# A graph kernel whose sum over three axes and scan terms move from TensorE to VectorE, with the turn of a batch reordered on ScalarE and TensorE

## The chip, the cores and the metric

The kernel runs on one core of one Trainium2 chip. The metric is the time of the whole program on the device in microseconds (us). A core has five engines that run side by side and wait for one another through semaphores: TensorE (PE: matmuls, and PEld for its weight loads), VectorE (DVE), ScalarE (ACT), GpSimd (POOL, which here issues the gathers) and SyncE (SP, which issues the other transfers). Each engine works through its own list of instructions in order.

## The reference

The reference has two layers on a graph of 12,500 nodes with 32 features and 200,000 edges, which are sorted by their destination `dst`.

```
x = layernorm(x + mean over the edges into a node of x[src])          # layer 0
R = relu(edge_weight * w1 + b1) @ w2 + b2                              # 384 numbers per edge
Y = spherical_harmonics(edge_attr_3)                                   # from the edge's direction
msg[e] = sum over (R, Y, features of src[e], constants)                # 8 scalars, 8 vectors of 3
x = layernorm(x + sum over the edges into a node of msg[e])           # layer 1
```

In layer 1 the 32 features of a node are 8 scalars and 8 vectors of three components, and so is a message. The kernel doesn't form `Y`. For each edge it has a rotation (`frame`, 3 by 3) that turns the edge's direction onto one axis. It rotates the gathered vectors into that frame, multiplies with `R` there, and rotates the message back. Rotating back is a sum over the three axes a of (message component a) times (row a of the frame).

## The kernel before

**Tiling.** The 200,000 edges lie as 128 partitions of 1564 edges; the columns are worked through in 98 batches (`BATCHES`) of `T` = 16 columns. A loop `layer1(i)` holds two batches, k = 0 and 1. Its batch is b. On each engine there is a function `layer1` that writes out by hand the order of its instructions for batch b, together with the rest of batch b-1 and the head start of batch b+1. Nothing else sets the order.

**A batch of layer 1.** GpSimd gathers the source nodes' features into `got[k]` (line 688), 16 gathers per batch. VectorE rotates them (lines 1659 to 1666) and ScalarE copies the scalars (842). TensorE transposes them (`turn_features`, 1002), ScalarE copies the result to `ft` (848), and TensorE spreads it in six steps (`spread_features`, 1018, S0 to S5). TensorE makes the radial numbers in six steps, always for the next batch (`radial`, 990, R0 to R5). All six use one pair of PSUM banks, `radial_slot`, so each waits until ScalarE has copied the last one to its SBUF room (`copy_radial`, 822). There is one room per step, and a room can be written again once VectorE has multiplied with it. VectorE multiplies in eight steps (`multiply`, 1645, m0 to m7). TensorE sums the products in four steps (`sum_products`, 1027).

**The turn of a batch.** After the last sum of batch b-1, ScalarE copies it to `summed_t` (`copy_summed`, 829), TensorE transposes it into the PSUM bank `messages` (`turn_messages`, 1037), VectorE copies the 8 scalars to `scalars_s` (1619) and makes the three products `back[a]` with the frame (`turn_back`, 1621). TensorE's `add_axes` adds the three by matmuls with the identity matrix (1043) and brings the scalars beside them (1045), into `terms2`. That is the same PSUM bank as `messages`, in another order: feature first, then column. VectorE adds the carry of the batch before (`carry`, 1437) and scans along the columns (`scan_terms`, 1442); ScalarE turns the runs (729), and they go to DRAM. On TensorE `add_axes` stands behind S0 and S1 and ahead of R1. On VectorE the scan stands between m3 and m4.

`Steps` numbers VectorE's own instructions: `mark` counts one, `settle` waits until all that were marked have ended. `STEPS` is the number of marks per turn of the loop. The line numbers are those of the kernel before.

Of the kernel before, what the change touches and what calls it, by code (L numbers as in the profile page):

```python
# [11 lines left out]
ALU = mybir.AluOpType  # L12
# [6 lines left out]
D = 32  # L19
MUL = 8  # L20
H = 64
RD = 6 * MUL * MUL
T = 16
COLS = 1568
CR = 1564
BATCHES = COLS // T
# [45 lines left out]
TL = CR - (BATCHES - 1) * T  # L72
# [15 lines left out]

STEPS = {"layer0": 8, "layer1": 16, "frames": 21}

# [15 lines left out]
def build_program(nc, x, src, dst, edge_attr, edge_weight, w1, b1, w2, b2, out):  # L106
    with ExitStack() as ctx:
# [3 lines left out]
        def sem(name):  # L111
            return ctx.enter_context(nc.semaphore(name))
# [93 lines left out]
        turned_in = [room[:, :, :, :, :].rearrange("p t a b v -> p t (a b v)") for room in f_along]  # L206
        scalars_s = f_across[1][:, :, :, :, :].rearrange("p t a b v -> p (t a b v)")[:, 0:T * MUL].rearrange("p (t u) -> p t u", u=MUL)
        summed_t = f_across[0][:, :, :, :, :].rearrange("p t a b v -> p (t a b v)")
# [67 lines left out]
        messages = ps_m[:, 0, :].rearrange("p (t o) -> p t o", o=D)  # L276
        terms2 = ps_m[:, 0, :].rearrange("p (o t) -> p o t", t=T)
        summed_p = ps_m[:, 1, :]
# [75 lines left out]
        back_ready = sem("back_ready")  # L354
        axes_summed = sem("axes_summed")
        frame_b_loaded = pair("frame_b_loaded")
# [348 lines left out]
        def _(act):  # L705
# [125 lines left out]
            def layer1(i, last=False):  # L831
                for k in range(2):
# [3 lines left out]
                    w = TL // QUAD * P if final else QUAD * P  # L836
                    if not first:
                        copy_summed(b - 1)
                    act.wait_ge(got2_landed[k], 16 * (T * i + n))
                    if not isinstance(b, int) or b > 1:  # L840
                        act.wait_ge(turned, b - 1)
                    act.copy(turned_in[k][:, 0:n, 0:MUL], got[k][:, 0:n, 0:MUL]).then_inc(f0_copied, 1)
                    copy_radial(b, UNITS - 1, w)
                    act.copy(idx[k][:, :], src_all[:, bass.ds((b + 2) * T, T)]).then_inc(idx_ready, 1)
                    act.wait_ge(turned, b + 1)
# [34 lines left out]
        def _(pe):  # L880
# [150 lines left out]
            def turn_messages(b, w=QUAD * P):  # L1031

                pe.wait_ge(summed_copied, b + 1)
                if not isinstance(b, int) or b > 0:
                    pe.wait_ge(scanned, BATCHES + b)
                for j in range(w // P):
                    mm = pe.transpose(ps_m[:, 0, j * P:(j + 1) * P], summed_t[:, j * P:(j + 1) * P], ident[:, :])  # L1037
                mm.then_inc(messages_ready, 1)

            def add_axes(b, n=T):  # L1040
                pe.wait_ge(back_ready, b + 1)
                for a in range(3):
                    pe.matmul(terms2[:, MUL:D, :].rearrange("p (u i) t -> p t i u", i=3)[:, 0:n], ident[:, :],  # L1043
                              back[:, a, 0:n], start=(a == 0), stop=(a == 2), skip_group_check=True)
                pe.matmul(terms2[:, 0:MUL, :].rearrange("p u t -> p t u")[:, 0:n], ident[:, :],
                          scalars_s[:, 0:n, :], start=False, stop=True, skip_group_check=True).then_inc(axes_summed, 1)

            def layer1(i, last=False):
                for k in range(2):
# [5 lines left out]
                    if not first:  # L1055
                        sum_products(b - 1, 3)
                        turn_messages(b - 1)
                    turn_features(b, k, w)
                    if not final:
                        radial(b + 1, 1 - k, 0, later)  # L1060
                    spread_features(b, k, 0, w)
                    spread_features(b, k, 1, w)
                    if not first:
                        add_axes(b - 1)
                    if not final:
# [32 lines left out]
            turn_messages(BATCHES - 1, TL // QUAD * P)  # L1098
            add_axes(BATCHES - 1, TL)

# [9 lines left out]
        def _(dve):  # L1110
# [499 lines left out]
            def turn_back(b, k, n=T):  # L1610

                dve.wait_ge(messages_ready, b + 1)
                if isinstance(b, int):
                    dve.wait_ge(frame_b_loaded[k], 16 * (b // 2 + 1))
                else:
                    dve.wait_ge(frame_b_loaded[k], 8 * (b - k + 2))
                if not isinstance(b, int) or b > 0:
                    dve.wait_ge(axes_summed, b)
                s.mark(dve.tensor_copy(scalars_s[:, 0:n, :], messages[:, 0:n, 0:MUL]))
                for a in range(3):  # L1620
                    ins = dve.tensor_tensor(back[:, a, 0:n], spread(messages[:, 0:n, MUL * (a + 1):MUL * (a + 2)], 2, 3),
                                            spread(frame_b[k][:, 0:n, :, a], 3, MUL), ALU.mult)
                    if a < 2:
                        s.mark(ins)
                ins.then_inc(back_ready, 1)

            def scan2(b, k):

                dve.wait_ge(axes_summed, b + 1)
                dve.wait_ge(masks2_ready, b + 1)  # L1630
                dve.wait_ge(runs_turned, BATCHES + b - 1)
                dve.wait_ge(scanned, BATCHES + b)
                carry(b, k, terms2)
                scan_terms(k, terms2)
# [69 lines left out]
```

## Time and profile before

| | |
|---|---|
| time, median of 3 runs | 3803.33 us (3798.77 to 3803.84) |
| profiled execution: its time | 3798.03 us |
| profiled execution: its span | 3796.3 us |
| TensorE busy | 3310.6 us (87%) |
| VectorE busy | 2762.8 us (73%) |
| GpSimd busy | 2786.3 us (73%) |
| ScalarE busy | 2061.5 us (54%) |
| mean granted clock of TensorE | 0.949 |

The span is the time from the first to the last instruction of the profiled execution. Busy shares are means over stages with different limits. Layer 0 with its nodes ends near 1590 us, layer 1's batches end near 3660 us, and the nodes of layer 1 follow. The clock is that granted to TensorE: 1.00 is 2.4 GHz, 0.50 is 1.2 GHz.

### The profile page before, as it was taken

What the parts mean: (1) busy time and instruction counts of PE and PEld (TensorE: products, weight loads), DVE (VectorE), ACT (ScalarE), POOL (GpSimd) and SP (SyncE); (2) the same over time, 40 slices, a digit from 0 to 9 for tenths busy, and PEclk for the clock granted to TensorE, in tenths of its full rate; (3) what the DMA queues carried; (4) which work ended last, traced back from release to release, by engine and by line L of the source; (5) the groups of instructions that cost most, each with busy time, mean ns of one, the idle gap of its engine ahead of it and who ended that gap; (6) DMA issues with size and microseconds to landing.
All of it is one profiled execution on the core that took longest, in us unless ns stands there. A gap on an engine that the chain in (4) does not pass through costs nothing.

```text
span 3796.3 us, 58108 instructions
## 1 busy us (share of the span) xinstructions
PE 3310.6 (87%) x17312; PEld 1902.1 (50%) x17312; DVE 2762.8 (73%) x3470; ACT 2061.5 (54%) x2391; POOL 2786.3 (73%) x2915
## 2 busy tenths in 40 slices
PE   4999999999999883399999999999999999999963
PEld 3898889898989783222323232333323232323232
DVE  5787877787878785467777777777777777777765
ACT  4777777776777660145454545454554545454520
POOL 6777777777777776677777777777777777777746
PEclk9999999999999995599999999999999999999975
DMA  4122222222122211122222222222222222222211
GB/s 100 39 57 41 52 43 43 50 44 54 40 55 43 50 48 29 39 57 53 62 55 59 55 59 55 59 58 56 62 52 62 55 59 54 59 55 59 57 28 26
DMA packets 188428, 197.65 MB, mean 52 GB/s; under 512 B 60241, under 2 KB 149427, under 8 KB 188085
## 3 DMA queue, kind: packets, MB, share of 16 engines
q1 hardware_dynamic: 95508, 149.13, 13.7%
q0 software_dynamic: 92832, 47.72, 9.7%
q14 instruction: 77, 0.63, 0.1%
q8 instruction: 11, 0.18, 0.0%
HBM read 134.02 MB, written 62.59 MB: 52 GB/s over the span
## 4 chain that ended last, share of the span: by engine, by line
PE 70%; ACT 12%; DVE 5%; POOL 5%; issue 5%; DMA 1%; SPq 0%; ACTq 0%; DVEq 0%; POOLq 0%
PE ps_r L940 19%; PE ps_r L990 17%; PE ps_m L1027 10%; PE ps_m L940 10%; PE ps_r L1018 8%; ACT prod_room L822 8%; POOL ngot L667 4%; DVE unit L1645 3%; PE ps_m L1037 2%; PE ps_r L1002 2%; ACT f_across L829 2%; PE ps_r L924 1%; ACT hot_s L739 1%; PE ps_m L1043 1%; ACT hot_s L742 1%
## 5 line engine op out<-in xcount | busy, mean ns | idle before, releaser
L688 POOL DMA_INDIRECT got<-x_d,idx x1564 | 1506.2, 963 | 530.6 <-issue 504.7
L822 ACT ACTIVATE prod_room<-ps_r,bias_col 128x1024 f32<-128x1024 f32 x392 | 435.9, 1112 | 780.0 <-PE ps_r L990 531.9
L940 PE MATMUL ps_r<-x_hi,hot_s 128*128 128x448 f32 x1974 | 741.6, 376 | 41.7 <-ACT hot_s L742 41.7
L1645 DVE TENSOR_TENSOR x_room<-radial_more,ps_r 128x1024 f32<-128x1024 f32 x392 | 475.0, 1212 | 384.0 <-PE ps_r L1018 252.3
L990 PE MATMUL ps_r<-hid,wc 64*128 64x512 f32 (+1 forms) x2352 | 669.8, 646 | 81.2 <-ACT prod_room L822 72.9
L940 PE MATMUL ps_r<-x_lo,hot_s 128*128 128x448 f32 x1974 | 733.0, 371 | 0.0
L739 ACT ACTIVATE hot_s<-rows,minus_row 128x512 fp32r<-128x512 f16 (+1 forms) x658 | 449.0, 764 | 244.0 <-PE ps_m L940 206.2
L1018 PE MATMUL ps_r<-ft,repeat 32*128 32x512 f32 (+1 forms) x2352 | 553.4, 639 | 1.1 <-ACT ft L848 0.6
L1645 DVE TENSOR_TENSOR unit<-prod_room,ps_r 128x1024 f32<-128x1024 f32 x392 | 451.1, 1213 | 106.9 <-PE ps_r L1018 102.0
L940 PEld LDWEIGHTS ps_r<-x_hi,hot_s 128*128 128x128 f32 x1974 | 378.3, 192 | 75.5 <-issue 43.0
L990 PEld LDWEIGHTS ps_r<-hid,wc 64*128 64x128 f32 x2352 | 178.8, 186 | 448.8 <-ACT prod_room L822 255.3
L940 PEld LDWEIGHTS ps_r<-x_lo,hot_s 128*128 128x128 f32 x1974 | 378.0, 192 | 32.7
L642 POOL DMA_INDIRECT got<-in_x_dram,idx_deep x322 | 310.5, 964 | 107.9 <-PE ps_r L940 42.7
L642 POOL DMA_INDIRECT f_across<-in_x_dram,idx_deep x331 | 314.3, 950 | 100.8 <-issue 42.0
L642 POOL DMA_INDIRECT f_along<-in_x_dram,idx_deep x326 | 315.0, 966 | 99.3 <-issue 40.2
L940 PE MATMUL ps_m<-x_hi,hot_s 128*128 128x448 f32 x987 | 362.0, 367 | 0.0
L940 PE MATMUL ps_m<-x_lo,hot_s 128*128 128x448 f32 x987 | 361.7, 366 | 0.0
L742 ACT ACTIVATE hot_s<-hot_s 128x3584 fp32r<-128x3584 f32 x94 | 336.1, 3576 | 3.0
L1018 PEld LDWEIGHTS ps_r<-ft,repeat 32*128 32x128 f32 x2352 | 148.0, 183 | 371.0 <-issue 150.3
L729 ACT COPY runs_t<-runs 128x512 f32<-128x512 f32 x196 | 210.0, 1071 | 133.8 <-DVE runs L1442 133.8
L667 POOL DMA_INDIRECT ngot<-run_d,pos x196 | 185.0, 944 | 111.5 <-issue 59.1
L1369 DVE TENSOR_TENSOR prod_room<-ps_r,hot_l 128x448 f32<-128x448 f32 x282 | 167.6, 620 | 118.8 <-PE ps_r L940 109.9
(203 smaller groups left out, 4438.4 us busy)
## 6 DMA issues: line engine op xcount, KB each, us to landing
hid<-weight_t SPq DMA_DIRECT2D x196, 256.0 KB
run_d<-runs_t SPq DMA_DIRECT2D x194, 256.0 KB
got<-x_d,idx POOLq DMA_INDIRECT x1564
rows<-code_d SPq DMA_DIRECT2D x47, 160.0 KB
frame_d<-x_sb SPq DMA_DIRECT2D x7, 1008.0 KB, 4.5
frame<-frame_d SPq DMA_DIRECT2D x98, 72.0 KB
frame_b<-frame_d SPq DMA_DIRECT2D x98, 72.0 KB
rows<-code_d SPq DMA_DIRECT2D x47, 128.0 KB
```

The costliest lines, as they stand in the source:

```text
L642: pool.indirect_dma_start(got_deep[k][:, t, :], None, x, bass.IndirectOffsetOnAxis(ap=idx_deep[q][:, k * T + t:k * T + t + 1], axis=0)).th ...
L667: pool.indirect_dma_start(ngot[c][:, j, :], None, table, bass.IndirectOffsetOnAxis(ap=pos[:, node_j:node_j + 1], axis=0)).then_inc(ngot_la ...
L688: pool.indirect_dma_start(got[k][:, t, :], None, x1_d, bass.IndirectOffsetOnAxis(ap=idx[k][:, t:t + 1], axis=0)).then_inc(got2_landed[k], 16)
L729: act.copy(runs_t[k][:, :, :], runs[k][:, :, :].rearrange("p f t -> p t f")).then_inc(done, 1)
L739: act.activation(hot_s[k][:, a, :, :], rows[k][:, :, :], ACT.Abs, bias=minus_row[:, a:a + 1]).then_inc(off_rows, 1)
L742: act.activation(hot_s[k][:, :, :, :], hot_s[k][:, :, :, :].bitcast(F32), ACT.Relu, bias=1.0, scale=-1.0).then_inc(hot_s_ready, 1)
L822: act.activation(radial_s[u][:, :, 0:w], radial_slot[:, :, 0:w], ACT.Identity, bias=bias_col[:, c:c + 1]).then_inc(radial_copied, 1)
L940: mm = pe.matmul(found[BANK_OF[k][g]], hot_s[k][:, a, g, :], part[:, a * LN * D:(a + 1) * LN * D], start=(a == 0 and n == 0), stop=(a == B ...
L990: mm = pe.matmul(radial_slot[:, t, 0:w], wc[half, c * P:(c + 1) * P], hid[k][half, :].rearrange("p (j c e) -> p j c e", c=2, e=P)[:, 0:w / ...
L1018: mm = pe.matmul(slot[:, t, 0:w], repeat[group, c, :], ft[group, 0:w], start=True, stop=True)
L1027: mm = pe.matmul(summed_p[t * D:(t + 1) * D, 0:w], to_feature[:, D - MUL - q * MUL:2 * D - MUL - q * MUL], product[q][t // 2][:, t % 2, 0: ...
L1645: dve.tensor_tensor(product[q][h][:, :, 0:w], radial_s[u][:, :, 0:w], spread_slot[(k + s_ + 1) % 2][:, :, 0:w], ALU.mult).then_inc(multipl ...
```

## The change

- `add_axes` goes. TensorE makes neither the sum over the axes nor the copy of the scalars, and the semaphore `axes_summed` goes with it.
- `terms2` moves from the PSUM bank to an SBUF tile (`f_across[1]`, which held `scalars_s`). VectorE copies the scalars into it directly, and adds the three products by two additions right behind them, ahead of m0. The second writes `terms2` with strides. Carry and scan read SBUF.
- The transpose of the messages waits for the products of the batch before (`back_ready`) instead of its scan.
- ScalarE: the copy of the sum (`copy_summed`) stands behind the copy of the scalar features and of the last radial step, instead of ahead of them.
- TensorE: R0 of the next batch stands ahead of both transposes, instead of behind them.

```diff
-STEPS = {"layer0": 8, "layer1": 16, "frames": 21}
+STEPS = {"layer0": 8, "layer1": 20, "frames": 21}
...
-        scalars_s = f_across[1][:, :, :, :, :].rearrange("p t a b v -> p (t a b v)")[:, 0:T * MUL].rearrange("p (t u) -> p t u", u=MUL)
+        terms2 = f_across[1][:, :, :, :, :].rearrange("p t a b v -> p (t a b v)").rearrange("p (o t) -> p o t", t=T)
...
-        terms2 = ps_m[:, 0, :].rearrange("p (o t) -> p o t", t=T)
...
@@ scalar, layer1
-                    if not first:
-                        copy_summed(b - 1)
                     act.wait_ge(got2_landed[k], 16 * (T * i + n))
...
                     act.copy(turned_in[k][:, 0:n, 0:MUL], got[k][:, 0:n, 0:MUL]).then_inc(f0_copied, 1)
                     copy_radial(b, UNITS - 1, w)
+                    if not first:
+                        copy_summed(b - 1)
                     act.copy(idx[k][:, :], src_all[:, bass.ds((b + 2) * T, T)]).then_inc(idx_ready, 1)
...
@@ tensor, turn_messages
                 if not isinstance(b, int) or b > 0:
-                    pe.wait_ge(scanned, BATCHES + b)
+                    pe.wait_ge(back_ready, b)
...
-            def add_axes(b, n=T):
-                pe.wait_ge(back_ready, b + 1)
-                for a in range(3):
-                    pe.matmul(terms2[:, MUL:D, :].rearrange("p (u i) t -> p t i u", i=3)[:, 0:n], ident[:, :],
-                              back[:, a, 0:n], start=(a == 0), stop=(a == 2), skip_group_check=True)
-                pe.matmul(terms2[:, 0:MUL, :].rearrange("p u t -> p t u")[:, 0:n], ident[:, :],
-                          scalars_s[:, 0:n, :], start=False, stop=True, skip_group_check=True).then_inc(axes_summed, 1)
...
@@ tensor, layer1
                     if not first:
                         sum_products(b - 1, 3)
+                    if not final:
+                        radial(b + 1, 1 - k, 0, later)
+                    if not first:
                         turn_messages(b - 1)
                     turn_features(b, k, w)
-                    if not final:
-                        radial(b + 1, 1 - k, 0, later)
                     spread_features(b, k, 0, w)
                     spread_features(b, k, 1, w)
-                    if not first:
-                        add_axes(b - 1)
                     if not final:
                         radial(b + 1, 1 - k, 1, later)
...
@@ vector, turn_back
-                if not isinstance(b, int) or b > 0:
-                    dve.wait_ge(axes_summed, b)
-                s.mark(dve.tensor_copy(scalars_s[:, 0:n, :], messages[:, 0:n, 0:MUL]))
+                s.mark(dve.tensor_copy(terms2[:, 0:MUL, :].rearrange("p u t -> p t u")[:, 0:n], messages[:, 0:n, 0:MUL]))
                 for a in range(3):
...
                 ins.then_inc(back_ready, 1)
+                s.settle()
+                s.mark(dve.tensor_tensor(back[:, 0, 0:n], back[:, 0, 0:n], back[:, 1, 0:n], ALU.add))
+                s.settle()
+                dve.wait_ge(back_ready, b + 1)
+                s.mark(dve.tensor_tensor(terms2[:, MUL:D, :].rearrange("p (u i) t -> p t i u", i=3)[:, 0:n],
+                                         back[:, 0, 0:n], back[:, 2, 0:n], ALU.add))
...
@@ vector, scan2
-                dve.wait_ge(axes_summed, b + 1)
                 dve.wait_ge(masks2_ready, b + 1)
+                s.settle()
```

## Rows read from the trace of the kernel before

**Rows 1.** The page: granted clock in 40 slices of the span, in tenths.
```profile
PEclk9999999999999995599999999999999999999975
```

**Rows 2.** One line's instructions (ns min/median/max, first and last start), and a group, 1900 to 3600.
```profile
L842 ACT COPY f_along<-got x81: 300/301/304, 1911.1 to 3582.3; 128x128 f32<-128x128 f32 x81
...
L688 POOL DMA_INDIRECT got<-x_d,idx x1307 | 1259.5, 964 | 441.0 <-issue 425.5 <-ACT f_along L842 15.5
```

**Rows 3.** Timeline, all engines, one batch: start, us, instructions, idle before and its releaser.
```profile
2516.40 0.56 DVE L1662 TENSOR_TENSOR part<-part 128x384 f32<-128x384 f32 x1
...
2517.07 0.65 PE L1037 MATMUL ps_m<-ident,f_across 128*128 128x128 f32 x4 [0.78 <-ACT f_across L829]
...
2518.13 1.47 DVE L1621 TENSOR_TENSOR back<-ps_m,frame_b 128x384 f32<-128x384 f32 x3
2518.26 1.13 PE L990 MATMUL ps_r<-hid,wc 64*128 64x512 f32 x4
2518.37 0.59 ACT L848 COPY ft<-ps_r 128x512 f32<-128x512 f32 x1
...
2519.32 1.14 PE L1018 MATMUL ps_r<-ft,repeat 32*128 32x512 f32 x8
...
2520.39 2.20 PE L1043 MATMUL ps_m<-back,ident 128*128 128x384 f32 x6
2520.66 4.61 DVE L1645 TENSOR_TENSOR unit<-prod_room,ps_r 128x1024 f32<-128x1024 f32 x4 [1.05 <-PE ps_r L1018]
...
2523.08 1.13 PE L990 MATMUL ps_r<-hid,wc 64*128 64x512 f32 x4 [0.27 <-ACT prod_room L822]
...
2524.34 1.11 ACT L822 ACTIVATE prod_room<-ps_r,bias_col 128x1024 f32<-128x1024 f32 x1 [1.31 <-PE ps_r L990]
...
2527.05 1.13 PE L990 MATMUL ps_r<-hid,wc 64*128 64x512 f32 x4
...
2535.01 1.13 PE L990 MATMUL ps_r<-hid,wc 64*128 64x512 f32 x4
...
2536.07 1.06 PE L1027 MATMUL ps_m<-x_room,to_feature 128*32 128x512 f32 x8
...
2537.28 0.59 ACT L829 COPY f_across<-ps_m 128x512 f32<-128x512 f32 x1 [2.33 <-PE ps_m L1027]
...
2537.99 0.65 PE L1037 MATMUL ps_m<-ident,f_across 128*128 128x128 f32 x4 [0.86 <-ACT f_across L829]
```

**Rows 4.** The chain that ended last, in order of time, two batches: start, us, what.
```profile
2521.92 1.12 ACT prod_room L822
...
2541.39 2.13 PE ps_m L1043 x6
```

**Rows 5.** Timeline, batch 0 of layer 1, TensorE.
```profile
1618.98 1.14 PE L1018 MATMUL ps_r<-ft,repeat 32*128 32x512 f32 x8
1622.70 2.08 PE L990 MATMUL ps_r<-hid,wc 64*128 64x512 f32 x4 [2.59 <-ACT prod_room L822]
...
1629.58 1.13 PE L990 MATMUL ps_r<-hid,wc 64*128 64x512 f32 x4
```

**Rows 6.** Groups of VectorE, 100 to 1600: busy us, mean ns of one, idle before.
```profile
L1413 DVE TENSOR_TENSOR x_sb<-unit,x_sb 128x224 f32<-128x224 f32 x7 | 4.2, 603 | 0.0
...
L1410 DVE TENSOR_TENSOR x_sb<-unit,x_sb 128x224 f32<-128x224 f32 x7 | 3.1, 437 | 0.0
```

**Rows 7.** Windows: length, busy of PE, PEld, DVE, ACT, POOL, granted clock, DMA share, GB/s.
```profile
1621.00:1622.00 1.00, 0.00 (x0) 0.00 (x0) 1.00 (x2) 0.46 (x1) 0.69 (x2) 0.99 0.04 5
```

**Rows 8.** Layer 0: timeline of TensorE, and windows (PE busy, clock, DMA share, GB/s).
```profile
1314.06 0.46 PE L940 MATMUL ps_r<-x_hi,hot_s 128*128 128x448 f32 x1 [2.98 <-ACT hot_s L742]
...
1314.00:1315.00 1.00, 0.94 (x4) 0.89 0.03 4
...
1318.00:1319.00 1.00, 1.00 (x6) 0.91 0.06 12
```

**Rows 9.** Timeline of GpSimd: one gather of layer 1.
```profile
2518.75 0.95 POOL L688 DMA_INDIRECT got<-x_d,idx  x1 [0.30 <-issue]
```

More of the change, by code:

```diff
@@ L354, in build_program @@
         back_ready = sem("back_ready")
-        axes_summed = sem("axes_summed")
         frame_b_loaded = pair("frame_b_loaded")
@@ L1098, in _ @@
             turn_messages(BATCHES - 1, TL // QUAD * P)
-            add_axes(BATCHES - 1, TL)
             pe.wait_ge(tail_ready[1], 1)
```

## The prediction

> **What bounds the kernel now.** I first read the page's line of the granted clock [rows 1]. It tells the stages apart: layer 0, a dip to half clock at the nodes, then layer 1, with the clock full from its second slice to its end. The diff touches layer 1 alone, so everything else is counted as unchanged. A tile that is copied once per batch gives the length of a batch: 80 steps between 1911.1 and 3582.3, 20.89 us each [rows 2]. Layer 1 has 98 batches. All but the last have another behind them, so I multiply by 97.
>
> Next comes the timeline of one batch [rows 3]. I measure from the start of the message transpose (M, line 1037) at 2517.07 to the next M at 2537.99, 20.92 us. R0 to R5 are the radial products (line 990), S0 to S5 the spreads (1018), m0 to m7 VectorE's multiplications (1645). R1 starts at M+6.01. R5 starts at R1+11.93, the last sum of products (line 1027) 1.06 behind it at R1+12.99, ScalarE's copy of that sum (829) at R1+14.20, and the next M at R1+14.91. The sum 6.01+14.91 gives the 20.92. TensorE is busy or one hop from busy nearly everywhere, so a reader of the page would call it the bound.
>
> The chain of waits shows what that hides [rows 4]. In one batch the way from S0 to R1 goes through m0 on VectorE and the radial copy on ScalarE; in the other it goes through the three axis matmuls. So two chains of equal length run between S0 and R1. R1 needs the PSUM slot that R0 filled; ScalarE empties it into the SBUF room that m0 must have read first. In [rows 3] this is S0 2519.32, m0 2520.66, R1 2523.08, with the copy at 2521.92 [rows 4] between them: 3.76 us. The axis matmuls lie wholly inside that wait. Batch 0 is the proof at hand: it has no axis matmuls, yet its S0 at 1618.98 is followed by R1 at 1622.70, 3.72 us, and TensorE stands idle 2.59 us in between [rows 5].
>
> **The change part by part.**
>
> *Axis matmuls and the scalars' matmul taken from TensorE.* They take from 2520.39 to about R1, 2.6 us, and leave 0 us of gain: 3.72 against 3.76. What was their place becomes an idle wait. S0 and S1 end about 1.07 us after S0's start (2519.32 to 2520.39).
>
> *R0 moved ahead of M, and ScalarE's last radial copy moved ahead of the copy of the sum.* In the kernel before, M waits for the sum's copy, until R1+14.91. In the new order R0 must first wait for ScalarE's copy of R5. From R1 (2523.08) its copy starts 1.26 later (2524.34) and takes 1.11. So R5's copy runs from R1+13.19 to R1+14.30, and R0 starts at R1+14.35. R0 and the next piece lie 1.06 apart (2518.26 to 2519.32), so M starts at R1+15.41. The sum's copy follows R5's on ScalarE, ends at about R1+14.9, and is covered. M is late by 15.41-14.91 = 0.50 us. Everything of the next batch hangs on M: the transposed messages start VectorE's part, whose m0 releases R1. The feature transpose queued behind M is late with it.
>
> *What the order gives back.* Without R0 between the feature transpose and S0, S0 starts once ScalarE has copied the features: M+1.30 (2518.37) plus 0.59 plus a hop of 0.12, as from the end of line 829 (2537.87) to M (2537.99). That is M+2.01 instead of M+2.25, and would allow m0 at M+3.35. But VectorE isn't free then.
>
> *Two additions on VectorE, and strided writes.* VectorE's three products start at M+1.06, in 1.48 us for three. I let the first addition start 0.06 before their end, M+2.48, since they overlap. It is of the kind and shape of line 1662, 0.56 us. It waits for the first to end; with an estimated hop of 0.06 the second starts at M+3.1. Its output is strided (64, 192 and 4 bytes in its loops), a form the layer doesn't have. Nearest are two multiplications of the frames with like inputs: 437 ns written densely, 603 with a stride [rows 6]. That is 0.74 ns for each of 224 elements; on 384 elements it is 0.28 us, so 0.84 us. The next instruction then starts some 0.08 before its end: m0 at M+3.86 instead of M+3.59, 0.27 us late. Bounds: dense price, 0 us; all 384 elements at the strided row's whole 2.7 ns each, 1.03 us, m0 0.46 late. The scalars' copy also gets a stride, at most 128 times 0.74 ns, which is inside that. I take 0.26. The old wait of VectorE before m0 (1.06 us) is what hides the rest; it is used up now. The scan reads SBUF instead of PSUM. It delays m4 at worst, which S2 doesn't wait for, so I give it nothing.
>
> The Trainium skill weighs against my stride price: "VectorE: DVE Perf Modes", section "The TRN2 errata", gives an fp32 tensor_tensor in SBUF as (N+151)/0.96 ns, 557 for 384 elements, with no term for strides. Row and formula agree for the dense form; by it alone the second addition costs 0.56 and the sum below falls by 26 us. "SBUF — State Buffer", section "Door 1: The DMA port swizzle", says on the other hand that each access to another 16-byte line pays, which the two rows of the frames bear out.
>
> *The clock.* Work done, R1 is now at M+6.01+0.26 = M+6.27, while S0 and S1 end at M+3.08. TensorE is idle for 3.2 us in every batch, and for 0.7 before S0. M's own wait, 0.86 us, is the longest of the batch before [rows 3]. Batch 0 shows what such a wait does: TensorE ran out of work at about 1620.1, the granted clock was at its upper level, 1.00 of 2.4 GHz, and fell at the end of the microsecond to 1622 [rows 7]. R1's four matmuls take 2.08 us there instead of 1.13, at 1.2 GHz; R2's at 1629.58 take 1.13 again [rows 5]. The same in layer 0: a wait of 2.98 us before 1314.06, fall at 1314.8, back near 1318.1 (0.89 and 0.91 are the means over the microseconds in which it changes) [rows 8]. So I expect a fall in nearly every batch, just as dense work starts. The price by rows: R1 to R2 took 1629.58-1622.70 = 6.88 at the low clock [rows 5], against 2527.05-2523.08 = 3.97 at the full one [rows 3]: 2.91 us. The shorter fall of layer 0 lasted 3.3 us, which costs half of it, 1.7. These are the bounds; both kinds should occur as the wait and the clock's changes slide against each other. I take 2.2, a little under their middle, since solid work follows R1.
>
> *The rest.* The last batch has its axis matmuls replaced by shorter additions, about 1 us saved once. GpSimd's gathers need 16 times 0.96+0.30, 20.2 us per batch [rows 2, 9], and stay under the new length. No DMA is moved past another; the frame reload waits for the same product as before.
>
> *Sum.* 0.50+0.26+2.2 = 2.96 us per batch, times 97 is 287, less 1 is 286. Before's profiled execution took 3798.03 us, with a span of 3796.3; the median of the runs is 5.3 higher. 3798+286+5 = 4089; I say 4085.
>
> **The rivals.**
>
> *A, the forecast.* Bounds per batch: 0.50+0+1.7 = 2.2 to 0.50+0.46+2.9 = 3.9, so 4015 to 4180. Chance 0.74.
>
> *B, the clock holds.* Then order and additions alone remain: 0.50 to 0.96, mid 0.76, times 97: 3850 to 3896, mid 3877. For it: batch 0's fall came soon after the clock had risen, and layer 1's steady batches never tested it. Against: the two falls [rows 7, 8] come with waits of 2.6 and 3.0. Chance 0.19. In "TensorE: Matmul & The Clock Gate", Part 1, the Trainium skill lets the clock fall only after an idle window; a wait with work on both sides wouldn't always be one, and by that the time would be B's. Batch 0's row speaks against it.
>
> *C, TensorE's load is the bound after all (the other side).* If R1 could follow S0 and S1 directly, a batch would lose 2.6 us and pay 0.50, and GpSimd's 20.2 would be the next limit: 0.69 times 97, 67 us less, 3736. It pays from the point where S0 to R1 gets under 3.76-0.5 = 3.26 us. Against: m0, copy and R1 are tied by the room that is reused, and batch 0's 3.72. Chance 0.04.
>
> *D, no change.* R0 ahead of M costs nothing, because ScalarE's copy of R5 ends before the last sum of products, and the additions fit into VectorE's old wait: 3803. Against: R5 starts only 1.06 ahead of that last sum, the copy needs 2.37 from R5's start. Chance 0.03.
>
> **How the numbers follow.** A measurement of this kernel tells about 0.2% from no change, 8 us. A's own range is 4015 to 4160. B has almost 2 in 10, and what lies above 4160 some more, so the range goes down to B: 3850 to 4160. Faster 0.04 (C), same 0.03 (D), slower 0.93 (A and B).
>
> **What would show each step.** In the profile after: no line 1043; TensorE idle about 3 us before R1, ended by the radial copy; R0 directly behind the last sum of products and M 1.06 behind R0; a batch of 23 to 24 us; two additions at 0.56 and about 0.84; the clock line at 7 to 9 tenths in the slices of layer 1, and means of line 990 well over 646 ns. If the batch is 21.4 to 21.9 with a full clock, B was right. The prediction is wrong at its root if R1 starts less than 5.5 us behind M, or if M doesn't wait for R0.

## The result and the profile after

The changed kernel takes 4203.55 us (median of 4 runs, 4199.66 to 4204.44), the kernel before, run beside it, 3802.89 (3798.77 to 3803.84). The ratio is 1.1061, 95% interval 1.1048 to 1.1074. The forecast had the direction right (slower, chance 0.93) and the time 119 us too low. 4203.55 lies above its range of 3850 to 4160.

The page of the changed kernel: busy time of each engine, the granted clock in 40 slices that answers to [rows 1], and two groups (busy us, mean ns | idle before them, releaser).

```profile
PE 3421.1 (81%) x16528; PEld 1825.5 (43%) x16528; DVE 2883.0 (69%) x3666; ACT 2060.2 (49%) x2391; POOL 2868.5 (68%) x2915
...
PEclk9999999999999756888888888888888888888875
...
L686 POOL DMA_INDIRECT got<-x_d,idx x1564 | 1584.8, 1013 | 844.6 <-issue 473.4
L988 PE MATMUL ps_r<-hid,wc 64*128 64x512 f32 (+1 forms) x2352 | 774.4, 740 | 385.5 <-ACT prod_room L820 352.4
```

Read the clock line first. From the second slice of layer 1 to its end it stands at 8 tenths, where [rows 1] has 9. TensorE's busy time went up by 110.5 us (3310.6 before) although the axis matmuls are gone. The kernel takes 400.7 us more in all, and the lower clock is spread over the whole of layer 1: that is the first reading. The radial products (line 988 here, 990 before) took 646 ns in the mean before and take 740 now, and 352.4 us of idle time in front of them end with ScalarE's copy.

One batch of the changed kernel in the timeline, to be laid beside [rows 3].

```profile
2522.18 0.66 PE L1035 MATMUL ps_m<-ident,f_across 128*128 128x128 f32 x4
...
2523.20 1.46 DVE L1607 TENSOR_TENSOR back<-ps_m,frame_b 128x384 f32<-128x384 f32 x3
...
2523.95 1.14 PE L1016 MATMUL ps_r<-ft,repeat 32*128 32x512 f32 x8 [0.67 <-ACT ft L846]
...
2524.57 0.55 DVE L1613 TENSOR_TENSOR back<-back 128x384 f32<-128x384 f32 x1
...
2525.16 0.81 DVE L1616 TENSOR_TENSOR f_across<-back 128x384 f32<-128x384 f32 x1
2525.47 1.20 POOL L686 DMA_INDIRECT got<-x_d,idx  x1 [0.31 <-issue]
2525.82 4.59 DVE L1637 TENSOR_TENSOR unit<-prod_room,ps_r 128x1024 f32<-128x1024 f32 x4
...
2528.22 2.08 PE L988 MATMUL ps_r<-hid,wc 64*128 64x512 f32 x4 [3.13 <-ACT prod_room L820]
...
2530.23 2.08 PE L1016 MATMUL ps_r<-ft,repeat 32*128 32x512 f32 x4
...
2530.72 1.88 POOL L686 DMA_INDIRECT got<-x_d,idx  x1 [0.30 <-issue]
...
2532.23 3.64 PE L1025 MATMUL ps_m<-unit,to_feature 128*32 128x512 f32 x16
...
2535.81 1.92 PE L988 MATMUL ps_r<-hid,wc 64*128 64x512 f32 x4
...
2539.03 1.13 PE L988 MATMUL ps_r<-hid,wc 64*128 64x512 f32 x4 [0.24 <-ACT prod_room L820]
...
2546.98 1.13 PE L988 MATMUL ps_r<-hid,wc 64*128 64x512 f32 x4 [0.30 <-ACT radial_more L820]
...
2548.04 0.66 PE L1035 MATMUL ps_m<-ident,f_across 128*128 128x128 f32 x4
```

R1 starts 6.04 us behind M (2522.18 to 2528.22), against 6.01 before. So the part of the batch that holds the two new additions hardly got longer. TensorE stands idle for 3.13 us ahead of R1 and then works at half speed: R1, S2 and the sixteen sums take 2.08, 2.08 and 3.64 us instead of 1.13, 1.13 and 1.92, and R2 is slow as well. M comes 1.06 behind R0, as forecast.

Windows of the same batch (columns as in [rows 7]) show when the clock fell and when it came back.

```profile
2526.00:2527.00 1.00, 0.00 (x0) 0.00 (x0) 1.00 (x2) 0.00 (x0) 0.70 (x2) 1.00 0.91 152
2527.00:2528.00 1.00, 0.00 (x0) 0.00 (x0) 1.00 (x2) 0.94 (x1) 0.92 (x1) 0.60 0.12 19
2528.00:2529.00 1.00, 0.78 (x2) 0.50 (x4) 1.00 (x2) 0.17 (x1) 0.77 (x1) 0.50 0.11 16
...
2537.00:2538.00 1.00, 1.00 (x6) 0.30 (x4) 0.00 (x0) 0.14 (x1) 0.70 (x2) 0.78 0.09 16
```

The granted clock is 1.00 (2.4 GHz) in the first window, falls in the second while TensorE waits, is 0.50 (1.2 GHz) in the third, and comes back between 2537 and 2538. That is some 10 us at the low level.

The chain that ended last, through the same stretch, runs over these slow matmuls, so that their time is paid for.

```profile
2525.86 1.18 DVE unit L1637
...
2527.05 1.12 ACT prod_room L820
...
2528.22 2.08 PE ps_r L988 x4
...
2532.30 3.57 PE ps_m L1025 x16
```

Two lengths describe a batch: M to R1 and R1 to the next M. Here they are for all kernels of this study, read from TensorE's timeline between 1900 and 3600 us, as means over the whole batches there (67 to 82, by kernel), with the mean granted clock of that stretch and the mean length of one gather.

| kernel | time, us | M to R1 | R1 to M | batch | clock | gather, ns |
|---|---|---|---|---|---|---|
| before | 3802.9 | 6.02 | 14.87 | 20.89 | 1.00 | 964 |
| after | 4203.6 | 6.04 | 19.01 | 25.04 | 0.84 | 1015 |
| e1_filler | 3864.0 | 6.06 | 15.41 | 21.47 | 1.00 | 1022 |
| e2_adds_only | 4093.3 | 6.10 | 17.80 | 23.89 | 0.86 | 1000 |
| e3_order_only | 3814.4 | 5.53 | 15.41 | 20.95 | 1.00 | 960 |
| e4_adds_only_filler | 3829.0 | 6.33 | 14.80 | 21.13 | 1.00 | 1003 |
| g1_filler_one | 3997.2 | 6.05 | 16.95 | 23.00 | 0.93 | 1019 |
| g2_filler_two | 3930.8 | 6.05 | 16.20 | 22.25 | 0.96 | 1016 |
| f1_room_before | 3767.2 | 5.68 | 14.87 | 20.55 | 1.00 | 961 |
| f2_room_adds_late | 3781.3 | 4.04 | 16.70 | 20.74 | 0.98 | 975 |
| f4_room_after | 3897.4 | 3.28 | 18.65 | 21.92 | 0.93 | 1010 |
| h1_dummy_sbuf | 3829.2 | 6.31 | 14.87 | 21.18 | 1.00 | 955 |
| h2_dummy_psum | 3828.5 | 6.30 | 14.87 | 21.18 | 1.00 | 954 |
| h3_scan_sbuf | 3812.6 | 6.08 | 14.87 | 20.95 | 1.00 | 992 |

The batch grew by 25.04-20.89 = 4.15 us. Times 97 that is 403, for 400.7 measured. Nearly all of it lies behind R1.

### The profile page after: what moved, and what is told of

The parts are those of the page before. It is cut to its first block, busy times and chain, and to the rows that moved or that the text cites. A ratio compares the mean times of both kernels' runs of the same rounds, so it can differ in the third digit from the quotient of the medians.

```text
span 4202.1 us, 56926 instructions
## 1 busy us (share of the span) xinstructions
PE 3421.1 (81%) x16528; PEld 1825.5 (43%) x16528; DVE 2883.0 (69%) x3666; ACT 2060.2 (49%) x2391; POOL 2868.5 (68%) x2915
## 4 chain that ended last, share of the span: by engine, by line
PE 65%; ACT 13%; DVE 10%; issue 6%; POOL 5%; DMA 1%; DVEq 1%; SPq 0%; ACTq 0%; POOLq 0%
PE ps_r L988 18%; PE ps_r L938 17%; PE ps_m L1025 10%; PE ps_m L938 9%; ACT prod_room L820 8%; PE ps_r L1016 7%; POOL ngot L665 4%; DVE unit L1637 3%; ACT radial_more L820 3%; DVE back L1607 3%; PE ps_m L1035 1%; PE ps_r L922 1%; DVE back L1613 1%; ACT hot_s L737 1%; ACT hot_s L740 1%
## 5 line engine op out<-in xcount | busy, mean ns | idle before, releaser
L686 POOL DMA_INDIRECT got<-x_d,idx x1564 | 1584.8, 1013 | 844.6 <-issue 473.4
L988 PE MATMUL ps_r<-hid,wc 64*128 64x512 f32 (+1 forms) x2352 | 774.4, 740 | 385.5 <-ACT prod_room L820 352.4
L1016 PE MATMUL ps_r<-ft,repeat 32*128 32x512 f32 (+1 forms) x2352 | 646.0, 724 | 70.0 <-ACT ft L846 66.0
L988 PEld LDWEIGHTS ps_r<-hid,wc 64*128 64x128 f32 x2352 | 199.3, 207 | 948.8 <-ACT prod_room L820 600.5
L1016 PEld LDWEIGHTS ps_r<-ft,repeat 32*128 32x128 f32 x2352 | 167.8, 204 | 473.7 <-issue 241.0
L1025 PE MATMUL ps_m<-unit,to_feature 128*32 128x512 f32 x1568 | 337.8, 1009 | 0.0
L820 ACT ACTIVATE radial_more<-ps_r,bias_col 128x1024 f32<-128x1024 f32 x196 | 217.2, 1108 | 114.7 <-PE ps_r L988 114.0
```

Source lines behind the costliest of these rows:

```text
L686: pool.indirect_dma_start(got[k][:, t, :], None, x1_d, bass.IndirectOffsetOnAxis(ap=idx[k][:, t:t + 1], axis=0)).then_inc(got2_landed[k], 16)
L820: act.activation(radial_s[u][:, :, 0:w], radial_slot[:, :, 0:w], ACT.Identity, bias=bias_col[:, c:c + 1]).then_inc(radial_copied, 1)
L988: mm = pe.matmul(radial_slot[:, t, 0:w], wc[half, c * P:(c + 1) * P], hid[k][half, :].rearrange("p (j c e) -> p j c e", c=2, e=P)[:, 0:w / ...
L1016: mm = pe.matmul(slot[:, t, 0:w], repeat[group, c, :], ft[group, 0:w], start=True, stop=True)
L1025: mm = pe.matmul(summed_p[t * D:(t + 1) * D, 0:w], to_feature[:, D - MUL - q * MUL:2 * D - MUL - q * MUL], product[q][t // 2][:, t % 2, 0: ...
```

## The experiments

The theory after the first look: the clock, which falls in the wait for R1, costs most of the time, and the orders and additions cost well under 1 us per batch. The rivals: the additions or the new orders cost the time themselves, as waits; or GpSimd's gathers, which have grown from 964 to 1015 ns, have become the limit.

**e1_filler: the changed kernel with three idle matmuls where the axis matmuls stood.** They write into the PSUM bank `messages`, which VectorE has read by then.

```diff
+            def fill(b, count):
+                pe.wait_ge(back_ready, b + 1)
+                for n in range(count):
+                    pe.matmul(ps_m[:, 0, 0:384], ident[:, :], same[:, n * 384:(n + 1) * 384], start=True, stop=True,
+                              skip_group_check=True)
...
                     spread_features(b, k, 1, w)
+                    if not first:
+                        fill(b - 1, 3)
```

> The changed kernel with three dummy matmuls per batch on TensorE in the place where the axis matmuls were (behind S0 and S1, released by the products; their output is read by nobody). Theory 1, the clock: the wait before R1 shrinks below 1.5 us, the granted clock stays at 1.00 through layer 1, and a batch takes 21.45 us (order 0.50, additions 0.05 over 20.9): 3855 us. Theory 2, the additions on VectorE, the SBUF scan and the new order cost the time by themselves and the clock only goes along: 4150 us or more.

Measured: 3864.01 us, ratio 1.016 (1.0143 to 1.0177). TensorE's timeline:

```profile
2510.84 1.14 PE L1016 MATMUL ps_r<-ft,repeat 32*128 32x512 f32 x8 [0.68 <-ACT ft L846]
2511.91 2.20 PE L1041 MATMUL ps_m<-same,ident 128*128 128x384 f32 x6
2515.12 1.13 PE L988 MATMUL ps_r<-hid,wc 64*128 64x512 f32 x4 [1.00 <-ACT prod_room L820]
```

R1 comes at the same place in the batch (M 2509.08, R1 2515.12: 6.04), the wait is filled by 2.2 us of useless work, and R1 takes 1.13 us again. Useless work makes the kernel 340 us faster. Between 1900 and 3600 us the granted clock is at its upper level throughout. So 4203.6-3864.0 = 339.5 us of the loss, 3.5 per batch, is the clock, and 62 us, 0.64 per batch, is all the rest.

**e2_adds_only: the changed kernel with both old orders.**

```diff
-                    if not final:
-                        radial(b + 1, 1 - k, 0, later)
                     if not first:
                         turn_messages(b - 1)
                     turn_features(b, k, w)
+                    if not final:
+                        radial(b + 1, 1 - k, 0, later)
...
+                    if not first:
+                        copy_summed(b - 1)
                     act.wait_ge(got2_landed[k], 16 * (T * i + n))
...
                     copy_radial(b, UNITS - 1, w)
-                    if not first:
-                        copy_summed(b - 1)
```

> The changed kernel with the old orders on ScalarE and TensorE: only the move of the sum to VectorE is left. Theory 1: M to R1 stays 6.04 us, TensorE waits some 2.6 us before R1 and the clock falls in most batches; 20.95 us plus 2.5 to 3.6 for the clock, 4050 to 4160 us. Theory 3, the changed order is what hurts: within 10 us of the kernel before, 3810.

Measured: 4093.27 us, 1.0767 (1.0749 to 1.0785). TensorE's timeline:

```profile
2507.39 2.08 PE L988 MATMUL ps_r<-hid,wc 64*128 64x512 f32 x4 [2.62 <-ACT prod_room L820]
...
2511.40 3.04 PE L1025 MATMUL ps_m<-unit,to_feature 128*32 128x512 f32 x16
2514.37 1.13 PE L988 MATMUL ps_r<-hid,wc 64*128 64x512 f32 x4
```

A wait of 2.62 us is enough. The clock falls in each of the 70 batches, R1 to R2 takes 6.98 us instead of 3.97, and the batch loses 17.80-14.87 = 2.93 us there, at most 17.87-14.87 = 3.00. The additions themselves move R1 by 6.10-6.02 = 0.08.

**e3_order_only: the kernel before with both new orders, the axis matmuls kept.** Its edit is that of e2_adds_only the other way round, made on the kernel before.

> The kernel before with the new orders on ScalarE and TensorE and the axis matmuls kept. Theory 1: the clock stays at 1.00; M starts 0.50 us later behind R1, but m0 can start at about M+3.3 since S0 is earlier, so M to R1 is 5.75: a batch of 21.15, 3829 us. Theory 3: most of the 400 us is here, 4100 us or more.

Measured: 3814.35 us, 1.0031 (1.0019 to 1.0044), against 3829 expected. R1 to M grew by 0.54, as forecast, but M to R1 shrank by 0.49. The timeline:

```profile
2503.79 0.66 PE L1037 MATMUL ps_m<-ident,f_across 128*128 128x128 f32 x4
...
2505.56 1.14 PE L1018 MATMUL ps_r<-ft,repeat 32*128 32x512 f32 x8 [0.68 <-ACT ft L848]
2506.63 2.20 PE L1043 MATMUL ps_m<-back,ident 128*128 128x384 f32 x6
...
2509.32 1.13 PE L990 MATMUL ps_r<-hid,wc 64*128 64x512 f32 x4 [0.27 <-issue]
```

Without R0 in front of it S0 starts at M+1.77 instead of M+2.25 (the forecast had M+2.01), and all behind it moves up. The forecast has this gift and says that it is lost because VectorE isn't free. That needs the additions: they hold m0 back. So neither part costs much alone (0.08 the additions, 0.06 the orders, or 0.13 by the two times), and together they cost 0.58 in e1_filler (0.64 by the times), because the additions stand where the orders give back.

**e4_adds_only_filler: e2_adds_only with the three idle matmuls of e1_filler.**

> Old orders, the sum on VectorE, and three dummy matmuls on TensorE where the axis matmuls were. Theory 1: clock 1.00, a batch of 20.9 to 20.95 us, 3803 to 3812 us: the same as before. Theory 2: the additions and the scan in SBUF cost by themselves, over 3850 us.

Measured: 3829.03 us, 1.007 (1.0053 to 1.0087), against 3803 to 3812 expected. The median batch is 20.94, as before, and the mean is 21.13. In four of the 80 batches M to R1 is 8.7 to 9.1 us long: VectorE waits for a late gather there, and the clock falls; in all others it is full. The group of gathers, and VectorE's waits (total us, times, longest), 1900 to 3600:

```profile
L686 POOL DMA_INDIRECT got<-x_d,idx x1285 | 1289.0, 1003 | 411.5 <-issue 401.4 <-ACT f_along L840 7.0 <-ACT idx L842 3.1
```

```profile
DVE part L1658 <- DMA got<-x_d,idx: 8.8, 25, 1.3
```

VectorE waits for gathered rows. Between two gathers lie 0.305 us, and about once in seven batches some 2 us, which the profile puts down to issue; in the mean that is 0.32. Sixteen gathers of 1.003 with 0.32 between them take 21.2 us, the mean batch: GpSimd has become the limit. The timeline shows where most of the 39 ns on 964 come from. About one gather per batch starts beside the scan and is long:

```profile
2560.64 1.23 DVE L1437 TENSOR_TENSOR_SCAN runs<-masks,f_across 128x512 f32<-128x512 f32 x1
2560.75 1.87 POOL L686 DMA_INDIRECT got<-x_d,idx  x1 [0.31 <-issue]
```

**g1_filler_one and g2_filler_two: e1_filler with one and with two idle matmuls** (`fill(b - 1, 1)` and `fill(b - 1, 2)`).

> The changed kernel with one dummy matmul per batch instead of three in TensorE's wait. Theory 1: the wait before R1 is still above 2 us, the clock still falls in most batches: 4050 to 4200 us. Rival: any work in the wait keeps the clock up, 3864 us as with three.

> The changed kernel with two dummy matmuls per batch in TensorE's wait; none gave 4204 us, one 3997, three 3864. Theory 1: the wait before R1 shrinks to about 1.7 us and the clock holds: 3864 to 3875 us. Rival (the loss goes down evenly with the work put in): about 3930 us.

Measured: 3997.18 (1.0505, 1.0484 to 1.0527) and 3930.81 (1.0342, 1.032 to 1.0363). With 0, 1, 2 and 3 idle matmuls the time is 4204, 3997, 3931 and 3864. R1's wait, 3.13 without filler, is 2.3 with one, 1.65 with two and 1.00 with three. I had expected one to save less (4050 or more) and two to hold the clock. Both were wrong: the loss goes away step by step. The batches tell how. Between 1900 and 3600 R1 to M is longer than 16 us, which means a fall, in 67 of 67 batches without filler, 44 of 73 with one, 30 of 75 with two and 0 of 78 with three. In the others it is 15.41 to 15.42. The length of the wait alone doesn't decide: with one idle matmul it is 2.3 us in the batches with a fall and in those without.

**f1_room_before: the kernel before with a second SBUF room for R0's copy**, so that the copy needn't wait for m0 of the batch before it.

```diff
+        radial_0 = [radial_s[0], spare_room[:, 0:2 * QUAD * P].rearrange("p (t e) -> p t e", t=2)]
...
-                if not isinstance(b, int) or b > 0:
+                if u == 0:
+                    if not isinstance(b, int) or b > 1:
+                        act.wait_ge(multiplied, len(PRODUCTS) * (b - 2) + 1)
+                elif not isinstance(b, int) or b > 0:
                     act.wait_ge(multiplied, len(PRODUCTS) * (b - 1) + (1, 2, 3, 4, 7, 8)[u])
-                act.activation(radial_s[u][:, :, 0:w],
+                act.activation((radial_0[k] if u == 0 else radial_s[u])[:, :, 0:w],
...
```

VectorE's multiplication reads the same room.

> The kernel before with a second SBUF room for the copy of R0, so that R1 no longer waits for m0. Theory 1 (two chains of equal length between S0 and R1): only the hop of 0.27 us before R1 goes, the axis matmuls still fill the way; a batch of 20.6 us, 3775 us. Rival: m0 and its copy alone set R1, and the second room takes 1 us or more: 3700 us.

Measured: 3767.15 us, 0.991 (0.9893 to 0.9926). It beats both kernels. The timeline:

```profile
2507.26 1.11 ACT L826 ACTIVATE prod_room<-ps_r,bias_col 128x1024 f32<-128x1024 f32 x1
2508.14 2.20 PE L1047 MATMUL ps_m<-back,ident 128*128 128x384 f32 x6
...
2509.55 3.48 DVE L1649 TENSOR_TENSOR unit<-prod_room,ps_r 128x1024 f32<-128x1024 f32 x3
2510.18 0.38 PE L1049 MATMUL ps_m<-f_across,ident 128*128 128x128 f32 x2
2510.49 1.13 PE L994 MATMUL ps_r<-hid,wc 64*128 64x512 f32 x4
```

ScalarE copies R0 at 2507.26, ahead of the multiplications, and R1 follows the axis matmuls with no wait. M to R1 falls from 6.02 to 5.68, 33 us over 97 batches, with 34 measured. Of the two chains between S0 and R1, the one through m0 is cut and the one through the axis matmuls is left, 0.34 us shorter. So the chain through m0 was the longer one, and removing the axis matmuls alone can gain nothing. GpSimd has next to no time left here either: 16 times 0.961+0.32 is 20.5, for a batch of 20.55.

**f4_room_after: the changed kernel with that second room.**

> The changed kernel with a second room for R0's copy. Theory 1: R1 follows S0 and S1, the wait moves to S2, which needs m1 at M+6.0, and shrinks to 2.1 us; if the clock holds 20.7 us by TensorE and 21.05 by GpSimd, 3815 to 3830 us; if it still falls in a part of the batches, up to 4000.

Measured: 3897.37 us, 1.0253 (1.0236 to 1.027). M to R1 falls to 3.28 us, 2.76 less than in the changed kernel, but the wait moves on: TensorE now stands 1.63 us ahead of S2, for VectorE's multiplication, with R1 between two waits, and the clock still falls in 54 of 77 batches (mean 0.93).

```profile
2517.38 1.13 PE L992 MATMUL ps_r<-hid,wc 64*128 64x512 f32 x4 [0.37 <-ACT prod_room L824]
2520.14 1.13 PE L1020 MATMUL ps_r<-ft,repeat 32*128 32x512 f32 x4 [1.63 <-DVE unit L1641]
```

**f2_room_adds_late: old orders, the second room, and the additions moved behind m3, ahead of the carry.**

```diff
@@ vector, turn_back
                 ins.then_inc(back_ready, 1)
-                s.settle()
-                s.mark(dve.tensor_tensor(back[:, 0, 0:n], back[:, 0, 0:n], back[:, 1, 0:n], ALU.add))
-                s.settle()
-                dve.wait_ge(back_ready, b + 1)
-                s.mark(dve.tensor_tensor(terms2[:, MUL:D, :].rearrange("p (u i) t -> p t i u", i=3)[:, 0:n],
-                                         back[:, 0, 0:n], back[:, 2, 0:n], ALU.add))
...
@@ vector, scan2: the same lines, ahead of its waits
```

> The sum on VectorE, but behind m3 instead of ahead of m0; old orders; a second room for R0's copy. R1 can follow S0 and S1 at about M+3.7, TensorE's longest wait is about 1.3 us before S2, the clock holds. By TensorE alone a batch would take 20.2 us, 3730 us. Theory 4 (GpSimd: additions and scan in SBUF stretch its gathers to 21.05 us per batch): 3810 to 3825 us, and VectorE waits for gathers.

Measured: 3781.28 us, 0.9946 (0.993 to 0.9963): faster than before, slower than f1_room_before, between what the two theories gave. The shortest batches take 20.12 us, which is what TensorE needs. The mean is 20.74, and sixteen gathers of 0.975 with 0.32 take 20.7: GpSimd has no time left, and VectorE waits for gathered rows 23 times. The clock has a part in it too: 16 of the 81 batches meet a stretch at the low clock and take 22.5 us in the mean, the other 65 take 20.3. The waits for TensorE that start these falls were not told apart into those that a late gather makes and others.

**h1_dummy_sbuf, h2_dummy_psum: does an addition stretch the gathers?** The kernel before, with two useless additions behind the three products. In the second kernel one input lies in PSUM.

```diff
                 ins.then_inc(back_ready, 1)
+                s.settle()
+                s.mark(dve.tensor_tensor(spare_room[:, 0:384], same[:, 0:384], same[:, 384:768], ALU.add))
+                s.settle()
+                s.mark(dve.tensor_tensor(spare_room[:, 0:384], same[:, 0:384], same[:, 384:768], ALU.add))
+                s.settle()
```

(`h2_dummy_psum`: `ps_m[:, 1, 0:384]` in place of `same[:, 384:768]`. `STEPS` of layer 1 is 20 in both.)

> The kernel before, unchanged on all other engines, with two dummy additions of 384 numbers on VectorE between its products and m0, both inputs and the output in SBUF, their output read by nobody. Theory 5 (VectorE instructions with two SBUF inputs stretch GpSimd's gathers): the mean gather goes from 964 to about 990 ns and a batch to 21.0 us, 3810 to 3825 us.

> The same two dummy additions, but one of their two inputs in PSUM; everything else as in the run with both in SBUF. Theory 5: the mean gather stays at 964 ns, and only the additions' delay of m0 is left, within 10 us of the kernel before. Rival: the gathers are stretched by any instruction of VectorE there, and both runs have the same mean.

Measured: 3829.24 (1.0082, 1.0065 to 1.0099) and 3828.46 (1.0084, 1.0067 to 1.01). The gathers take 955 and 954 ns in the mean, not 990. But the mean hides what happens. The same place in a batch, first with both inputs in SBUF, then with one in PSUM:

```profile
2533.72 0.56 DVE L1629 TENSOR_TENSOR spare_room<-same 128x384 f32<-128x384 f32 x1
2533.93 1.16 POOL L688 DMA_INDIRECT got<-x_d,idx  x1 [0.31 <-issue]
```

```profile
2533.75 0.55 DVE L1629 TENSOR_TENSOR spare_room<-same,ps_m 128x384 f32<-128x384 f32 x1
2533.97 0.94 POOL L688 DMA_INDIRECT got<-x_d,idx  x1 [0.30 <-issue]
```

With both inputs in SBUF 56 gathers start beside the second addition and take 1.15 us in the mean; with one in PSUM 55 do, and none takes more than 0.96. So an addition does stretch the gather beside it, by 0.2 us, and where its input lies decides. The mean doesn't show it because VectorE's rotation (line 1659 before, 1664 here), which has two SBUF inputs as well, meets the gathers at other moments: in the kernel before 116 gathers start beside it and take 1.15 us in the mean, in h1_dummy_sbuf 102 with 0.97.

Both kernels lose some 32 us against the 3797.1 of the kernel before on the same chip, where 10 at most were expected of h2_dummy_psum, and both lose the same, since GpSimd has time to spare in a batch of 21.18. In h1_dummy_sbuf m0 starts at M+3.89, 0.30 late, with a wait of 0.30 us behind the second addition, which is the third `settle`'s. R1 moves with m0, from M+6.02 to M+6.31, though the axis matmuls are in place: it is m0's chain that sets R1.

**h3_scan_sbuf: does the scan?** The kernel before, its scan reading a constant SBUF tile in place of `terms2` in PSUM. The message sums of layer 1 are left out by that.

```diff
                 carry(b, k, terms2)
-                scan_terms(k, terms2)
+                scan_terms(k, same[:, 0:D * T].rearrange("p (o t) -> p o t", t=T))
```

> The kernel before with one thing changed: the scan's second input is a constant SBUF tile of the same shape instead of terms2 in PSUM, so both its inputs lie in SBUF (the message sums of layer 1 are therefore left out of the result). Theory 6 (a gather that is issued while a scan with two SBUF inputs runs waits for its end): the mean gather goes from 964 to about 1000 ns, one in 16 takes up to 1.9 us, and since a batch has 20.9 us and the gathers then need 20.9 to 21.0, the time goes up by 0 to 15 us. Rival (the stretched gathers of the changed kernel come from its strided writes or its additions): the mean stays at 964 ns, 3800 us.

Measured: 3812.61 us, 1.0025 (1.0015 to 1.0034). The group of gathers 1900 to 3600, to be laid beside [rows 2]:

```profile
L688 POOL DMA_INDIRECT got<-x_d,idx x1298 | 1287.4, 992 | 414.0 <-issue 403.9 <-ACT f_along L842 8.2 <-ACT idx L844 1.8
```

and the timeline of one scan:

```profile
2509.34 0.95 POOL L688 DMA_INDIRECT got<-x_d,idx  x1 [0.30 <-issue]
2510.53 1.23 DVE L1442 TENSOR_TENSOR_SCAN runs<-masks,same 128x512 f32<-128x512 f32 x1
2510.59 1.93 POOL L688 DMA_INDIRECT got<-x_d,idx  x1 [0.30 <-issue]
```

This gather, which starts beside a scan with two SBUF inputs, takes 1.93 us. In the kernel before, with one input in PSUM, it takes 0.94:

```profile
2546.42 1.22 DVE L1442 TENSOR_TENSOR_SCAN runs<-masks,ps_m 128x512 f32<-128x512 f32 x1
2546.43 0.94 POOL L688 DMA_INDIRECT got<-x_d,idx  x1 [0.30 <-issue]
```

There 77 gathers start beside the scan, and all take 0.94 to 0.95. With two SBUF inputs the long ones end 0.75 us behind the end of the scan, wherever they started in it, as if they had waited for it. One operand moved makes the stretch beside the scan. In the changed kernel, between 1900 and 3600 us, 68 gathers start beside the scan and take 1.82 us in the mean, and 58 start beside the strided addition and take 1.25, for 0.94 elsewhere. Of the added time three quarters is the scan's and one quarter the addition's.

## Why the direction was right and the size wrong

**Removing the axis matmuls gains nothing: right.** M to R1 is 6.04 against 6.02. No run takes away the axis matmuls alone, but f1_room_before and h1_dummy_sbuf show that m0's chain sets R1 and that the chain through the axis matmuls is 0.34 us shorter.

**Order, +0.50: right.** R1 to M at the full clock is 15.41 in e1_filler and e3_order_only, for 15.41 forecast (14.87 before, in the mean). That the order's gift is lost to VectorE's work is also shown: in e3_order_only, without the additions, it is kept.

**Additions and strides, +0.26: too much, by 0.2.** Each part was a little off in one direction. VectorE's groups, 1900 to 3600, by form:

```profile
L1616 DVE TENSOR_TENSOR f_across<-back 128x384 f32<-128x384 f32 x68 | 55.1, 810 | 2.3
L1613 DVE TENSOR_TENSOR back<-back 128x384 f32<-128x384 f32 x67 | 36.7, 547 | 0.0
```

The strided addition takes 810 ns, for 840 worked out from [rows 6], so the stride has its price, and the Trainium skill's formula without one, quoted in the prediction from "VectorE: DVE Perf Modes", misses it: it gives 557, near what the dense form takes (547). The prediction says that row and formula agree for the dense form. That holds for the row of 384 elements, and not for the one of 224, where the formula gives 391 and [rows 6] has 437. But m0 starts at M+3.64, not M+3.86. The first addition starts at M+2.39 rather than 2.48, the second 0.59 behind it rather than 0.62, it is 0.03 shorter, and m0 starts 0.15 ahead of its end rather than 0.08 (2525.82, end 2525.97). These four make the 0.22. This error, some 20 us over the batches, hid a part of the one in the clock's price.

**The clock, +2.2, bounds 1.7 to 2.9: this step failed, by its size.** That a fall would come in nearly every batch was right: 67 of 67. Its price was wrong, 3.60 us by the table (19.01-15.41), 3.5 by the two times. I took the dearest fall to be batch 0's, 2.91 from R1 to R2 more than at the full clock, and a value below the middle since "solid work follows R1". In e2_adds_only, with the old orders, that bound is just what every batch pays, 2.93. In the changed kernel there are two kinds: 44 of the 67 batches have R1 to M at 18.48 to 18.66, 3.1 to 3.25 more than 15.41, and 23 have 19.81 to 19.84, 4.4 more. In the second kind, which is the batch shown, R2 too runs at the low clock (1.92 us), and R2 to R3 takes 3.22 instead of 2.43. I had let no fall reach past R2. Why the changed kernel has the long kind and e2_adds_only doesn't isn't settled. It has a longer wait ahead of R1 (3.13 to 2.62) and a second one of 0.67 ahead of S0, but nothing here was run that varies these alone.

The sum again with measured terms: 0.54+0.02+3.60 = 4.16 per batch, 403 us. With 3.6 in place of 2.2 the forecast would have been 4085+136 = 4221, less 97 times 0.2 for the additions 4202.

**Rival B, the clock holds (0.19): it fell.** Yet it is the right time for the kernel whose clock is held: e1_filler's 3864 lies in its 3850 to 3896. The rule of "TensorE: Matmul & The Clock Gate", Part 1, in the Trainium skill, that the clock falls after an idle window, would have led there. The trace doesn't bear it out as a guard: in e2_adds_only and the changed kernel waits of 2.6 and 3.1 us, with work on both sides, were enough in every batch.

**Rival C, TensorE's load is the bound: wrong, and f2_room_adds_late shows what it lacked.** With R1 freed from m0, batches of 20.12 appear on TensorE, but the gathers fill the mean batch of 20.74, and the clock falls in some. C's limit of 20.2 for GpSimd left out the gaps of 2 us: with 0.32 for the mean gap it is 20.5, and C's time near 3770. f1_room_before, the fastest kernel here, takes 3767.

**GpSimd's floor of 20.2: it stayed under the new batch, and is itself too low.** At a batch of 25 us the gathers hide: between 1900 and 3600 us GpSimd waits 263 us for VectorE to free a room. But they grew: 16 times 1.015+0.30 is 21.0. I gave the scan's new place nothing, on the ground that S2 doesn't wait for m4. h3_scan_sbuf shows that its price is on another engine, and e4_adds_only_filler that it counts as soon as the batch is short. The Trainium skill has a rule that fits, in "SBUF — State Buffer", section "Who interferes with whom": a VectorE instruction with two SBUF inputs contends with a GpSimd instruction that reads SBUF, for a port pair that one of them holds for the whole instruction. The trace agrees for the scan (1.82 us in the mean for 0.94) and for the dense addition (1.15, and 0.94 with one input in PSUM). The gather reads its indices `idx` in SBUF. That it is this port they wait for is not shown by any run.

## What to carry to other kernels

Before taking work off TensorE, ask what the engine will do in its place. If the answer is a wait of some microseconds with dense work behind it, the work may have been what held the clock, and the test is cheap: put useless matmuls back and see. Where a trace of before offers a price for a clock fall, don't take the dearest for the upper edge: here 2.91 was about the price of the cheaper of two kinds. Check how far along the dense work the low clock could reach. When an operand moves from PSUM to SBUF, look at what runs beside the reader on other engines, not only at the reader. And where a mean over many instructions doesn't move, look at the single ones that the change could touch.

## What the runs showed of the hardware that was not expected

- A granted clock of 0.50 lasted about 10 us (2527.2 to 2537.4) with TensorE at work nearly throughout after its wait, in about a third of the batches.
- The clock isn't held or lost as a whole: with waits of 2.3 and 1.65 us ahead of R1 it fell in 44 of 73 and in 30 of 75 batches.
- A scan with two SBUF inputs holds up GpSimd's indirect transfer beside it: 1.87 and 1.93 us instead of 0.94. With one input in PSUM it doesn't.
- An addition of 384 elements does the same on a smaller scale: 1.15 us in the mean with both inputs in SBUF (h1_dummy_sbuf), 0.94 with one in PSUM (h2_dummy_psum), and 1.25 beside the longer, strided addition of the changed kernel.
- A strided fp32 addition of 384 elements takes 0.81 us, a dense one 0.55.
